# Reading every fourth piece of the adjacency by a narrowing GpSimd transfer

## What is computed

```python
# layer 0: symmetric-normalised GCN, two weight matrices for the two halves of the nodes
A = adj + eye; deg = A.sum(1); A = A * rsqrt(deg)[:, None] * rsqrt(deg)[None, :]
x = x + leaky_relu(A @ concat([h[:2048] @ Wr, h[2048:] @ Wd]) + bias, 0.01)
# layer 1: two graph convolutions
g = relu(concat([h, adj @ h], 1) @ W1);  x = x + relu(concat([g, adj @ g], 1) @ W2)
# layer 2: GCN with degree normalisation
x = x + relu((A_norm @ h) @ W.T + b)
# layer 3: attention over the edges, positive and negative softmax
x = x + elu(concat([softmax(e | adj) @ h, -softmax(-e | adj) @ h], 1) @ wtrans)
```

## Time and profile before

| what | us |
|---|---|
| median of 3 runs | 2165.55 (2163.09 to 2169.38) |
| the profiled execution | 2167.66 |
| its span | 2165.9 |
| PE busy in the span | 2056.9 (95%) |
| ACT busy | 1450.5 (67%) |
| DVE busy | 1404.4 (65%) |
| POOL busy | 2.1 |

### The profile page before, as it was taken

One profiled execution on the slowest core, in us unless ns is written; L12 is line 12 of the kernel. 1 busy time (PEld: TensorE's weight loads), 2 busy tenths in 40 slices (PEclk: granted clock), 3 DMA queues, 4 the chain that ended last, 5 costly groups with the idle time before them and its releaser, 6 DMA issues.

```text
span 2165.9 us, 26711 instructions
## 1 busy us (share of the span) xinstructions
PE 2056.9 (95%) x10489; PEld 1492.4 (69%) x10560; DVE 1404.4 (65%) x2230; ACT 1450.5 (67%) x1763; POOL 2.1 (0%) x12
## 2 busy tenths in 40 slices
PE   2699899999989999999999989999999999999998
PEld 2577787555545555554555478888888888888887
DVE  5778585000024242424546999999999999999674
ACT  5666677546546655556655578888887878797963
POOL 0000000000000000000000000000000000000000
PEclk9999999999999999999999999999999999999999
DMA  9988324201040212321118573435443536252200
GB/s 334 330 317 294 123 108 146 69 20 39 20 133 14 78 39 78 114 79 59 56 33 273 196 222 142 183 136 179 151 181 138 197 111 225 102 215 78 102 20 10
DMA packets 102686, 289.35 MB, mean 134 GB/s; under 512 B 45216, under 2 KB 52128, under 8 KB 86048
## 3 DMA queue, kind: packets, MB, share of 16 engines
q1 hardware_dynamic: 97184, 279.24, 37.5%
q10 hardware_dynamic: 5376, 8.39, 1.2%
HBM read 245.63 MB, written 33.58 MB: 129 GB/s over the span
## 4 chain that ended last, share of the span: by engine, by line
PE 87%; DVE 5%; ACT 4%; DMA 3%; issue 2%; SPq 0%; POOL 0%; DVEq 0%; ACTq 0%
PE ps L1685 40%; PE ps L1596 30%; PE ps L1613 6%; PE ps L1473 5%; PE ps L1655 2%; ACT work L577 1%; DMA work<-in_adj_t 1%; PE ps L1535 1%; ACT big L577 1%; PE ps L1522 1%; PE ps L1565 1%; DMA feat<-in_adj 1%; DMA work<-in_w_gcn 1%; DMA feat<-in_adj_t 0%; DVE stat L1231 0%
## 5 line engine op out<-in xcount | busy, mean ns | idle before, releaser
L577 ACT ACTIVATE work<-big 128x1024 bf16<-128x1024 uint8 x450 | 469.8, 1053 | 315.9 <-PE ps L1596 306.1
L1596 PE MATMUL ps<-work,feat 128*128 128x512 bf16 x3001 | 663.4, 380 | 10.2 <-DVE feat L1157 4.3
L1596 PEld LDWEIGHTS ps<-work,feat 128*128 128x128 f16 x3072 | 300.8, 98 | 369.5 <-issue 8.2
L1685 PE MATMUL ps<-big,work 128*128 128x257 f32 x2048 | 452.1, 382 | 4.9 <-ACT work L889 4.9
L1685 PE MATMUL ps<-big 128*128 128x257 f32 x2048 | 449.4, 380 | 2.2 <-ACT big L889 2.2
L1685 PEld LDWEIGHTS ps<-big,work 128*128 128x128 f32 x2048 | 389.4, 191 | 61.0 <-issue 4.8
L1685 PEld LDWEIGHTS ps<-big 128*128 128x128 f32 x2048 | 388.5, 190 | 58.1 <-ACT big L889 3.1
L1473 PE MATMUL ps<-feat,work 128*128 128x256 f16 x2048 | 234.2, 275 | 19.1 <-ACT work L577 7.6
L1473 PEld LDWEIGHTS ps<-feat,work 128*128 128x128 bf16 x2048 | 200.1, 98 | 51.3 <-ACT work L577 9.6
L881 ACT ACTIVATE big<-feat,uv_sb 128x512 f32<-128x512 f32 x256 | 163.3, 710 | 22.5 <-PE ps L1685 22.5
L881 ACT ACTIVATE work<-feat,uv_sb 128x512 f32<-128x512 f32 x256 | 163.5, 713 | 16.5 <-PE ps L1685 15.9
(11 more groups left out here) (153 smaller groups left out, 1342.7 us busy)
## 6 DMA issues: line engine op xcount, KB each, us to landing
big<-in_adj_t SPq DMA_DIRECT2D x64, 1024.0 KB, 4.9
feat<-in_adj SPq DMA_DIRECT2D x56, 1024.0 KB, 6.9
work<-in_adj_t SPq DMA_DIRECT2D x86, 512.0 KB, 6.2
feat<-in_adj_t SPq DMA_DIRECT2D x42, 512.0 KB, 6.5
h_spill<-work SPq DMA_DIRECT2D x32, 512.0 KB, 3.6
feat<-h_spill SPq DMA_DIRECT2D x32, 512.0 KB, 4.0
x_spill<-work SPq DMA_DIRECT2D x24, 512.0 KB, 2.6
work<-in_x SPq DMA_DIRECT2D x16, 512.0 KB, 5.3
```

Source lines behind the costliest of these rows:

```text
L577: return nc.scalar.activation(out_, in_, ACT.Copy, **kw)
L1596: ins = mm(ps[:, bank + f, :], parts[:, j, h, f * P:(f + 1) * P], stage[:, g % STAGES, jj, :], start=(fresh and h == 0), stop=(end and h = ...
L1685: ins = mm(ps[:, 4 * s + t, 0:YW], quads[k % RING][:, jj, t * P:(t + 1) * P], Yb[:, j, s, :], start=(j == 0), stop=(j == NT - 1), skip_gro ...
```

## The change

Pieces with `g % 4 == 1` (four of a chunk, 32 in all) are no longer asked for by SP and take no slot. GpSimd asks for them (`load_narrow`), from the same float32 source straight into their place in `adj8`, which holds bytes, so the transfer itself narrows four bytes to one. ACT casts only `g % 4` 0 and 2, DVE still 3. The other 96 pieces share the six slots (`held` lists them). A narrowing transfer waits for DVE's count of the group nine before it, and for the landing of the narrowing transfer two before it, so at most two are under way. DVE's count waits for its landing (`narrow_in`) where it waited for ACT's cast.

```diff
--- before.py
+++ after.py
@@ -175,6 +175,7 @@
 
 
         piece_in = [sem(f"piece_in{q}") for q in range(NQ)]
+        narrow_in = [sem(f"narrow_in{q}") for q in range(2)]
         small_in, weights_in = sem("small_in"), sem("weights_in")
         x_in_s = [sem(f"x_in{s}") for s in range(2)]
         parts_in = [sem(f"parts_in{c}") for c in range(NC)]
@@ -303,27 +304,34 @@
 
         def by_act(g):
 
-            return g % 4 != 3
+            return g % 4 in (0, 2)
+
+        def by_dma(g):
+
+            return g % 4 == 1
 
         def casts_of(n):
 
-            return n // 4 * 3 + n % 4 + 1 if by_act(n) else n // 4 + 1
+            return n // 4 * 2 + n % 4 // 2 + 1 if by_act(n) else n // 4 + 1
+
+        held = [n for n in range(NC * GROUPS) if not by_dma(n)]
 
         LAST = (NC - 1) * GROUPS
 
         def piece_slot(n):
 
+            k = held.index(n)
             if n < LAST - GROUPS:
-                return n % NQ
-            return (1, 2, 3, 4, 5)[(n - LAST + GROUPS) % 5] if n < LAST else (2, 3, 4, 1)[(n - LAST) % 4]
+                return k % NQ
+            return (1, 2, 3, 4, 5)[(k - held.index(LAST - GROUPS)) % 5] if n < LAST else (2, 3, 4, 1)[(k - held.index(LAST)) % 4]
 
         def piece_turn(n):
 
-            return sum(piece_slot(m) == piece_slot(n) for m in range(n + 1))
+            return sum(piece_slot(m) == piece_slot(n) for m in held if m <= n)
 
         def piece_before(n):
 
-            return max(m for m in range(n) if piece_slot(m) == piece_slot(n))
+            return max(m for m in held if m < n and piece_slot(m) == piece_slot(n))
 
 
         @block.sync
@@ -344,7 +352,7 @@
 
 
             load_x(x_in, 0, 0)
-            for g in range(NQ):
+            for g in held[:NQ]:
                 load_piece(0, g)
             sp.dma_start(w_sb[:, 0:KB[0], :], w_gcn.rearrange("(k p) f -> p k f", p=P)).then_inc(weights_in, 16)
             load_x(x_in, 1, 1)
@@ -353,11 +361,13 @@
 
             def pieces(c, first=0):
                 for g in range(first, GROUPS):
+                    if by_dma(g):
+                        continue
                     n = piece_before(c * GROUPS + g)
                     sp.wait_ge(cast_act if by_act(n) else cast_dve, casts_of(n))
                     load_piece(c, g)
 
-            pieces(0, NQ)
+            pieces(0, held[NQ])
             for c in range(1, NC):
                 pieces(c)
                 sp.wait_ge(h0_done, c * TPC)
@@ -561,7 +571,22 @@
                 nc.gpsimd.affine_select(out=eye[:, :], in_=eye[:, :], compare_op=ALU.not_equal, fill=1.0, base=0,
                                         pattern=[[-1, P]], channel_multiplier=1).then_inc(consts_ready, 1)
 
+            def load_narrow(c, g):
+
+                k = c * GROUPS // 4 + g // 4
+                wait(pool, count_step, c * GROUPS + g - 9)
+                wait(pool, narrow_in[k % 2], 16 * (k // 2))
+                t = g % 2 * PANELS
+                nc.gpsimd.dma_start(adj8[:, g * PANELS:(g + 1) * PANELS, c * CH:(c + 1) * CH],
+                                    adj_t[c, g // 2, :, t:t + PANELS, :]).then_inc(narrow_in[k % 2], 16)
+
+            for g in range(1, GROUPS, 4):
+                load_narrow(0, g)
             for n in range(2):
+                if n == 1:
+                    for c in range(1, NC):
+                        for g in range(1, GROUPS, 4):
+                            load_narrow(c, g)
                 pool.wait_ge(gown_ready, n + 1)
                 nc.gpsimd.partition_all_reduce(g_all, g_own, P, bass.bass_isa.ReduceOp.max).then_inc(gall_ready, 1)
 
@@ -640,7 +665,7 @@
                         part, summed_at = {4: (part3, PART2_SUMMED), 5: (part0, PART3_SUMMED), 6: (part4, PART4_SUMMED)}[c]
                         act.wait_ge(blk_used, summed_at)
                         if c == 6:
-                            n = max(m for m in range(LAST) if piece_slot(m) == 0)
+                            n = max(m for m in held if m < LAST and piece_slot(m) == 0)
                             act.wait_ge(cast_act if by_act(n) else cast_dve, casts_of(n))
                         copy(part[:, :, :], ps[:, 4:6, :].rearrange("p b (t f) -> p (b t) f", t=2)).then_inc(half_saved, 1)
 
@@ -1095,7 +1120,7 @@
             for c in range(NC):
                 for g in range(GROUPS):
                     n = c * GROUPS + g
-                    if not by_act(g):
+                    if not by_act(g) and not by_dma(g):
                         dve.wait_ge(piece_in[piece_slot(n)], piece_turn(n) * 16)
                         nc.vector.tensor_copy(adj8[:, g * PANELS:(g + 1) * PANELS, c * CH:(c + 1) * CH],
                                               piece[piece_slot(n)]).then_inc(cast_dve, 1)
@@ -1125,7 +1150,11 @@
                     if c > 0:
                         for m, pair in staged_at(c, g):
                             stage_pair(m, pair)
-                    dve.wait_ge(cast_act if by_act(g) else cast_dve, casts_of(n))
+                    if by_dma(g):
+                        k = n // 4
+                        dve.wait_ge(narrow_in[k % 2], 16 * (k // 2 + 1))
+                    else:
+                        dve.wait_ge(cast_act if by_act(g) else cast_dve, casts_of(n))
                     count(c, g)
                     if g * PANELS // TPC == c:
                         dve.wait_ge(count_step, n + 1)
```

## The result

The changed kernel takes 2176.99 us (median of 8 runs, 2174.91 to 2178.99) against 2167.1 of the kernel before beside it (8 runs): ratio 1.0046, interval 1.0037 to 1.0055. That is 9.9 us slower where 8 faster was forecast. The profiled execution has a span of 2175.8 us, 9.9 more than before.

What follows compares the result with a forecast made beforehand. Slots were taken to hold back the reading in chunks 1 to 7, with transfer engines and PE as next limits. 2167.66 - 10 (reading) + 2 (start) = 2159.7, by the median 2157.6 us; range 2147 to 2205.

Steps and rivals of the forecast that it cites:

- the start: Chunk 0: GpSimd's late first request and the reduction behind four transfers; +2 us, kept 0 to +9.5.
- The landing: Chunk 0, piece 1: 6.3 us to landing, moving DVE's count of group 1 from 13.95 to about 19.5 us.
- The cover: Chunk 0: requests of about 7 MB last to 21 us, so transfer engines idle a few us at most.
- The reduction: Chunk 0, GpSimd, behind four transfers: needs 1.65 or 7.04 us; DVE takes its result between 27.8 and 33 us.
- The lag would be made up in chunk 1: Chunk 1: DVE recovers its delay from chunk 0, being busy 18.4 of 28.4 us.
- the smaller number of slots (five, four) now serves 12 pieces instead of 16: Chunks 6 and 7: serving 12 pieces with fewer slots stays inside these chunks' bounds; no separate cost in the sum.
- The gain of narrowing: Chunks 1 to 7: fewer pieces through the slots shorten the reading; 10 us, kept 0 to 19.8.
- the sign named for the slots: Chunks 1 to 7: SP's waits for casts far below 147 us would show the forecast right.
- The bound of 19.8 us: Chunks 1 to 7: most to gain, each chunk limited by the larger of transfer engines' and PE's busy time; 19.8 us.
- Slow narrowing: Transfer engines: narrowing costs f times a plain read, deciding from about 1.6; +33, 2198 at f = 2; chance 0.27.
- Too few under way: Chunks 1 to 7: two narrowing transfers fall short; at 16 us a landing some +27, 2193; chance 0.11.
- The swallowed gain: Chunks 4 to 6 keep PE's 7.3 us idle, chunk 0 costs 6 to 9 us; 2164, same; chance 0.16.

Runs made afterwards that it cites:

- e1: Kernel before with only pieces 1, 5, 9 and 13 of chunk 0 narrowed by GpSimd, last chunks' slots oldest first; 2176.90 us, ratio 1.0057.
- e4: Changed kernel plus one unused reduction over the partitions on GpSimd, ahead of the four transfers of chunk 0; 2175.07 us.
- e3: Changed kernel with the slot order of chunk 7 altered from 2, 3, 4, 1 to 3, 4, 1, 2; 2172.91 us.
- e2: Kernel before with narrowing in chunks 1 to 7 only (28 pieces), last chunks' slots oldest first; 2160.20 us, ratio 0.9975.
- e10: Kernel before with every fourth piece narrowed from piece 13 on, all asked for behind the first reduction, aligned slot orders; 2160.02 us, ratio 0.9971.
- e7: Kernel before with 28 pieces of chunks 1 to 7 asked for by GpSimd as plain float32 transfers, not narrowed; 2172.41 us, ratio 1.0024.
- e9: Kernel before with only pieces 1 and 5 narrowed, both asked for ahead of the first reduction; 2170.99 us, ratio 1.0023.

## Why the prediction was wrong

It forecast 2157.6 us and a gain; 2176.99 is inside its wide range (to 2205) but on the other side, and not by the mechanism of either slower rival.

The step that failed is **the start**, taken at +2 us with a bound of +9.5. It is 10.9 us at the first count of chunk 1, and e1, which has only this part of the change, is 10.6 us slower in all (8.9 in its profiled execution). More than 5 us was the prediction's own sign that the start was taken too lightly. Four parts of that step were wrong:

- *The landing.* Piece 1 was given 6.3 us, the median of all plain pieces. It took 8.5, with SP's transfers on the same engines; in e4, where they had run dry, the first narrowed piece landed after 4.7. DVE's count of group 1 came at 21.3 us, not 19.5.
- *The cover.* "About 7 MB, which at 331 GB/s last to 21 us": 331 is the mean of the first 110 us. In chunk 0 the engines moved 401 to 410 GB/s at a full share, so by my estimate (7 MB at 405 GB/s) the cover ended some 4 us sooner. The rates of chunk 0 stood in the earlier trace rows, but the table by chunk that I built my view on began at 34 us, and chunk 0, where the change first acts, was not in it.
- *The reduction.* The working had the 7 us of preparation as a possibility, but counted it so that it ended at 33 us; it starts only when GpSimd reaches it, behind the fourth request (27.0 us), took 8.7 us and ended at 35.7. DVE's use of it came at 36.1 instead of 27.8 to 33.
- *The lag would be made up in chunk 1*, because DVE is busy only 18.4 of 28.4 us. DVE's idle time was the wrong measure: these chunks wait on slots, landings and the round trips between ACT and PE, and DVE's free time shortens none of them. In e1 chunk 1 takes 28.2 us where it took 27.5 before. Some of the lag was made up even so, in chunks 2 to 4: e1 has 3.6 us less in chunks 1 to 4 than the kernel before. How much of it other executions make up is open, since the medians keep 10.6 of the 11.5 us.

The second failed step is "the smaller number of slots (five, four) now serves 12 pieces instead of 16; that is inside the bounds of these chunks". The order of slots was written for 16 pieces, and with 12 its seam puts two neighbours into one slot. It costs 3.0 us in chunk 6 by the trace and 4 to 5 in all (e3). It stood in the diff for anyone who carried the two tuples through to their seam.

**The gain of narrowing** was taken at 10 us and is about 6 (e2 and e10). The way to it was only half right. The transfers' free time in chunks 1 to 3 is used up, but the sign named for the slots, SP's waits for casts far below 147 us, did not come: from 34 to 240 us SP waits 156 us for casts in e2. What fell were ACT's waits for landings. The bound of 19.8 us took the larger of the transfers' and PE's busy time and left out the third limit, the round trips of the earlier trace rows. By PE's idle time chunk 1 gave 2.2 us of its 4.0, chunk 2 all of its 1.9, chunk 7 1.6 of its 4.2, and chunks 3 to 6 0.7 of their 9.7. In chunks 4 to 6 PE is idle 6.8 us in e2 where it was 7.3, and by the prediction's own sign that means that slots did not hold them. Of the 24.5 free us of the transfers, 28 x 0.27 = 7.6 went to f = 1.18; that this cost time is not shown.

**The rivals.** Slow narrowing: f = 1.18, below its threshold of 1.6. Too few under way: the median landing is 8.2 us and the longest 10.2, below 13.4. The swallowed gain was right on chunks 4 to 6, where PE's short waits stayed, and nearest on the start, "6 to 9 us in full". Its figure of 2164 does not follow from its terms: 6 us gained and 6 to 9 paid give 2166 to 2169.

```profile
L580 POOL DMA_DIRECT2D big<-in_adj_t x32: 716/716/1081, 12.8 to 221.8; - x32
...
DMA to landing us min/median/max: 4.1/8.2/10.2
```

The same rows bear on whether requests of GpSimd and work of DVE hold each other up: a request takes 0.72 us in the median and 1.08 at most, and DVE's casts take 691 and 687 ns where the earlier trace rows has 690 and 688. No sign of either holding up the other can be seen at four requests a chunk; the sum had left it out. The Trainium skill (SBUF — State Buffer, the "DVE blocks DMA" trap) warns that GpSimd cannot write its requests while DVE runs in a two-port mode; nothing of a size that matters here is seen of it. That the second asking queue brings no rate of its own agrees with e7, which was not faster and where both queues need the same 1.5 us a piece.

The parts put together, by the medians: start +10.6 (e1), slots +4.1 (e3), narrowing in chunks 1 to 7 -6.1 (e2), sum +8.6; measured +9.9 with an interval of 8.0 to 11.9. The 1.3 us between them are within the scatter of the medians.

## What to carry to other kernels

Look at the stretch where a change first acts, with its own rates and its own idle times; a mean over the rest says nothing about a start that runs at full transfer rate. When requests are put on an engine that until now did little, write down what else stands in its list and who waits for that; a one-time preparation counts from where it stands in the list. When the number of pieces in a rotation changes, carry the rotation through every seam. Before two single traces are compared by the length of a stretch, look at the granted clock of each: here it moved a chunk by up to 3 us, while the idle time of PE, on which the chain runs here, showed what the change had done.

## What the runs showed of the hardware

The first reduction over the partitions on GpSimd needs 7.0 to 8.3 us of its own before it starts (7.45 in e4), and 8.7 to 9.7 behind four requests; a later one needs none (0.04 us behind the request in e4). A transfer that narrows float32 to bytes from 2 KB rows takes 1.18 times the engine time of a plain one for the same source bytes (1.76 against 1.49 us for 512 KiB), and lands 8.2 us after it is asked for in the median, with others under way, against 6.3 for a plain one (6.7 for SP's pieces in the changed kernel, 6.2 for the plain ones of GpSimd in e7). A plain transfer asked for by GpSimd costs the transfer engines the same as one of SP. At the start, GpSimd's identity tiles come only at 12.3 us (11.1 to 13.1 by kernel), 11.2 us of it idle, and the first piece asked for behind them was there at 20.8 us (e9) and 21.3 us (changed kernel). The granted clock was at its lower level for some 7 us around the turn to chunk 2 in e10 (its mean is 0.75, 0.50 and 0.90 in the three stretches of 4 us from 58 us on) and likewise in e2 (0.69, 0.50, 0.96), where it fell again later (0.68 in 74 to 78, 0.57 in 90 to 94 us). PE was busy 1.0 us of 54 to 58 us in e2, and not at all in 58 to 62 us in e10.
